# Three reduced-precision products in place of one full one for 44 down projections, the router inside the actor's matrix, an opening that runs by tiles, and GpSimd's follow-up steps planned later

## What is computed

```python
probs = softmax(einsum('bsh,eh->bse', x, router_w))              # 8 experts
a_h = gelu(einsum('bsh,ah->bsa', x, actor_w1) + actor_b1)        # 50 hidden
sampled_k = argmax(clip(a_h @ actor_w2.T + actor_b2, -30, 30)) + 1
rank = argsort(argsort(-probs))
scores = where(rank < sampled_k[..., None], probs, 0.0)
for e in range(8):                                               # I = 336
    g = einsum('bsh,ih->bsi', x, gate_w[e])
    u = einsum('bsh,ih->bsi', x, up_w[e])
    y = einsum('bsi,hi->bsh', silu(g) * u, down_w[e])
    out = out + scores[..., e:e + 1] * y
```

## Time and profile before

| | us |
|---|---|
| median of 3 runs | 499.86 |
| lowest, highest | 499.83, 501.45 |
| the profiled execution | 500.62 |
| its span in the profile | 498.8 |
| PE busy in it | 484.0 |
| DVE, POOL, ACT busy in it | 294.1, 292.1, 243.4 |

### The profile page before, as it was taken

One profiled execution on the slowest core, in us unless ns is written; L12 is line 12 of the kernel. 1 busy time (PEld: TensorE's weight loads), 2 busy tenths in 40 slices (PEclk: granted clock), 3 DMA queues, 4 the chain that ended last, 5 costly groups with the idle time before them and its releaser, 6 DMA issues.

```text
span 498.8 us, 6344 instructions
## 1 busy us (share of the span) xinstructions
PE 484.0 (97%) x2035; PEld 340.1 (68%) x2035; DVE 294.1 (59%) x695; ACT 243.4 (49%) x437; POOL 292.1 (59%) x307
## 2 busy tenths in 40 slices
PE   7798899999999899999999999999999999999997
PEld 7676767677666666676676676667676676666666
DVE  3538343746768795497937985469763334623232
ACT  3185837457624874248742756326671344232221
POOL 4346779338868485464563656365563646655653
PEclk9899999999999999999999999999999999999999
DMA  8700000000000000000000000000000000000000
GB/s 240 237 0 2 0 1 1 0 1 1 1 1 1 1 0 1 0 1 1 0 1 1 0 2 0 1 0 24 0 1 0 1 23 0 0 1 21 1 1 21
DMA packets 7932, 7.36 MB, mean 15 GB/s; under 512 B 732, under 2 KB 7772, under 8 KB 7900
## 3 DMA queue, kind: packets, MB, share of 16 engines
q1 hardware_dynamic: 7900, 6.97, 4.6%
HBM read 5.91 MB, written 1.05 MB: 14 GB/s over the span
## 4 chain that ended last, share of the span: by engine, by line
PE 81%; DVE 2%; ACT 1%; issue 1%; POOL 0%; ACTq 0%; DVEq 0%
PE bank L1157 26%; PE bank L1007 15%; PE bank L1009 14%; PE bank L1008 14%; PE bank L1195 3%; PE bank L1187 1%; PE bank L1111 1%; PE bank L1027 1%; PE bank L1165 1%; PE bank L1207 1%; PE bank L1119 1%; PE bank L1145 1%; PE bank L1098 1%; PE bank L1097 0%; PE bank L1085 0%
## 5 line engine op out<-in xcount | busy, mean ns | idle before, releaser
L574 POOL TENSOR_TENSOR t<-t,sl 128x512 f32<-128x512 f32 x105 | 136.0, 1299 | 109.8 <-DVE t L953 93.4
L691 ACT ACTIVATE sl<-bank 128x512 f32<-128x512 f32 x168 | 99.3, 597 | 150.0 <-PE bank L1009 143.5
L1157 PE MATMUL bank<-t,WD 128*128 128x512 f32 x328 | 162.7, 591 | 0.0
L953 DVE TENSOR_TENSOR t<-bank,sbc 128x512 f32<-128x512 f32 x105 | 72.4, 690 | 93.7 <-PE bank L1009 92.5
L1007 PE MATMUL bank<-xhF,WGh 128*128 128x512 f32 x168 | 103.8, 618 | 3.0 <-ACT sl L691 2.2
L574 POOL TENSOR_TENSOR t<-t,sbc 128x512 f32<-128x512 f32 x63 | 81.9, 1326 | 11.2 <-ACT sbc L685 7.9
L1157 PEld LDWEIGHTS bank<-t,WD 128*128 128x128 f32 x328 | 61.8, 188 | 25.1 <-issue 13.0
L953 DVE TENSOR_TENSOR t<-bank,sl 128x512 f32<-128x512 f32 x63 | 42.8, 685 | 54.7 <-ACT sl L691 24.3
L1007 PE MATMUL bank<-xhF,WUh 128*128 128x512 f32 x168 | 66.5, 396 | 1.3 <-DVE t L953 1.3
L1009 PE MATMUL bank<-xhF,WGl 128*128 128x512 f32 x168 | 66.3, 395 | 0.0
L1009 PE MATMUL bank<-xhF,WUl 128*128 128x512 f32 x168 | 66.0, 393 | 0.0
(11 more groups left out here) (191 smaller groups left out, 636.8 us busy)
## 6 DMA issues: line engine op xcount, KB each, us to landing
stage<-in_gate SPq DMA_DIRECT2D x7, 192.0 KB, 6.1
stage<-in_up SPq DMA_DIRECT2D x7, 192.0 KB, 6.3
WD<-in_down SPq DMA_DIRECT2D x7, 192.0 KB, 6.2
X<-in_x SPq DMA_DIRECT2D x4, 256.0 KB, 5.5
out<-X SPq DMA_DIRECT2D x3, 256.0 KB, 2.3
raw<-in_small SPq DMA_DIRECT2D x1, 388.0 KB, 4.6
out<-X SPq DMA_DIRECT2D x2, 128.0 KB, 1.9
raw<-in_small SPq DMA_DIRECT2D x1, 192.0 KB, 2.7
```

The lines of the kernel that those rows point to most:

```text
L574: pool.tensor_tensor(t2[k % NT2][:, :], t2[k % NT2][:, :], by[:, :], ALU.mult).then_inc(a_done, 1)
L691: act.activation(sl[k % NSL][:, :], bank[k % 2][:, :], ACT.Silu).then_inc(silu_done, 1)
L953: dve.tensor_tensor(t2[k % NT2][:, :], bank[2 + k % 2][:, :], by[:, :], ALU.mult).then_inc(t2_done, 1)
L1157: pe.matmul(OACC[:, :], WD[:, c, :], t2[k % NT2][:, :], start=(c == 0), stop=(c == CH - 1 or k == TAIL[0] - 1))\
```

## The change

**Split down projections.** For 44 of the 168 chunks `down` becomes three float32r matmuls. `plan` picks them in a new function, `halves`: from chunk 54 on (`SPLIT_FROM`), outside `TAIL`, where its running estimate of DVE's load is under a limit and POOL is not too far behind. ACT copies the finished `t2` into `ah` in float32r (step `ah`, 4 buffers), DVE writes the rest `t2 - ah` over `t2`, which it sees as float32r under the name `t2r` (step `al`), and `down` waits for that. The weights are split once, in 7 pieces from slot 27 on: ACT makes `WDh`, POOL makes `WDl` (step `wd`). By block the 44 are 0, 0, 4, 2, 4, 5, 12 and 17; the longest runs of neighbouring chunks are 98 to 101, 127 to 133 and 143 to 163.

**Router in the actor's matrix.** The router's 8 columns move into the columns 64 to 71 of the actor's matrix, whose first 50 are used. `route` is the three wide matmuls alone. A new step `rt` turns the 8 rows of logits into columns by four transposes. The 8 small matmuls, the copies of the router and DVE's sum of three parts go.

**Opening by tiles.** PE waits for `xn` tile by tile. `y` of batch 0 writes four banks and DVE adds each tile when it is there. The first half of `xhF` goes through bank 3 and is copied and split ahead of the second. Chunk 0 starts with the two products that need `xhF` alone. The sums of squares stand ahead of the product beside them, in a bank of their own, and `head_mask` is done half before the first `rstd` and half after.

**POOL's follow-ups later.** What POOL does for `stats`, `ass` and `actk` becomes steps of their own, `rstd`, `apow` and `sx`, that the tables place up to two slots later.

```diff
+SPLIT_FROM, WD_FROM = 2 * CH + 12, CH + 5
...
-F0_STEPS = [(0, "route"), (1, "inner", 0), (2, "rexp"), (3, "inner", 1), (3, "rsum"), (5, "rrank"), (5, "tanh"),
+F0_STEPS = [(0, "route"), (1, "inner", 0), (1, "rt"), (2, "rexp"), (3, "inner", 1), (4, "rsum"), (5, "rrank"), (5, "tanh"),
...
+    def halves(k):
+        room = debt[0] < DEBT_ACT and dve_load[0] < DVE_ROOM + DVE_LOAD["uk"] and pool_free[0] < k + POOL_LEAD
+        for j in split:
+            if ("al", j) not in done and slot_of.get(("ah", j), last) < k:
+                add(("al", j))
+                debt[1] += COST["al"][2]
+        j = seen[0]
+        while j < len(um_end) and um_end[j] + AH_LAG <= k and slot_of["um", j] < k:
+            weights = slot_of.get(("wd", j % CH // WCH), last) + 1 < k
+            if j >= SPLIT_FROM and j not in TAIL and weights and room:
+                split.append(j)
+                add(("ah", j))
...
+                if kind == "ah":
+                    act.wait_ge(a_done, k + 1)
+                    if i >= NAH:
+                        act.wait_ge(down_done, split[i - NAH] + 1)
+                    act.activation(ah[i % NAH][:, :], t2[k % NT2][:, :], ACT.Copy).then_inc(ah_done, 1)
...
+                if kind == "al":
+                    dve.wait_ge(ah_done, i + 1)
+                    dve.tensor_tensor(t2r[k % NT2][:, :], t2[k % NT2][:, :], ah[i % NAH][:, :].bitcast(F32),
+                                      ALU.subtract).then_inc(al_done, 1)
...
                 if kind == "route":
                     m = turn(t)
+                    wh, wl = swide(1)
+                    three(m[:, :], wh, wl, xh[:, :], xl[:, :]).then_inc(m_full[t % 3], 1)
+                if kind == "rt":
+                    wait_free(pe, turn_of["route", n])
+                    m = turn(t)
                     for i in range(NT):
-                        pe.matmul(m[:, o:o + 2 * E], xh[:, a], router[:, :], start=True, stop=True)
-                        r = pe.matmul(m[:, o + 2 * E:o + 3 * E], xl[:, a], router[:, 0:E], start=True, stop=True)
+                        r = pe.transpose(m[:, i * E:i * E + E], xa[R0:R0 + E, i * P:i * P + P], ident[R0:R0 + E, R0:R0 + E])
...
+                    if k in split_at:
+                        r = three(OACC[:, :], WDh[:, c, :], WDl[:, c, :], ah[i % NAH][:, :], t2r[k % NT2][:, :],
+                                  start=(c == 0), stop=(c == CH - 1 or k == TAIL[0] - 1))
```

More of the change, by code:

```diff
@@ L178, in plan, with bank_free @@
     um_end, downs, block_end = [], [0], []
+    split, seen = [], [0]
+    dve_load = [0.0]
+    slot_of = {}
+    wds = [("wd", j) for j in range(CH // WCH)]
+    def bank_free(by):
+        return by in done and (by[0] != "byx" or slot_of[by] < k)
     def ready(s):
@@ L224, in products @@
             j = downs[0]
-            if j < len(um_end) and um_end[j] + AFTER_POOL <= k and (j % CH or j == 0 or block_end[j // CH - 1] + OACC_REST < k):
+            if j in split:
+                due = slot_of.get(("al", j), last) + 1 < k
+            else:
+                due = j < seen[0] and um_end[j] + AFTER_POOL <= k
+            if due and (j % CH or j == 0 or block_end[j // CH - 1] + OACC_REST < k):
                 add(("down", j))
@@ L244, in plan @@
                 th[0] -= th[0] <= k
+        halves(k)
         products(k, 2)
+        if wds and k >= WD_FROM and k % 2:
+            add(wds.pop(0))
+            debt[0] += 0.5
         pe = 2.2
@@ L265, in plan @@
         debt = [max(0.0, act - pe), max(0.0, dve - pe)]
-    assert not any(th[1] for th in threads)
+        dve_load[0] = max(0.0, dve_load[0] - pe)
+    assert not any(th[1] for th in threads) and not wds
     while downs[0] < last:
```

244 lines of the change are left out of this document (168 added, 76 removed).

## The result

The changed kernel takes 503.85 us (median of 6 runs, 502.20 to 503.98), the kernel before 499.85 (499.76 to 501.45): a ratio of 1.0059, 95% interval 1.0044 to 1.0074. The forecast was 487.0, in a range from 483.0 to 491.5. The change makes the kernel 0.6% slower, and the forecast is 17 us off.

What follows compares the result with a forecast made beforehand. PE's work was taken to bound the kernel from chunk 0 on, after an opening chain. 500.62 - 7.3 (splits) - 3.7 (router) - 2.7 (opening) + 0.9 (waits) = 487.8 us, 487.0 against the median; range 483 to 491.5.

Steps and rivals of the forecast that it cites:

- Splits, -7.3 on PE: Down projections of 44 chunks: three float32r matmuls cost 0.69 us against 0.86 for the full down, 7.3 us less.
- the dense stretches don't gain: Rival, chance 0.12: um and al hinder each other, slots of 32 neighbouring chunks stay at 2.24 us, time 492.3.
- POOL goes first: Rival, chance 0.05: in dense stretches POOL gets SBUF ahead of DVE each time, slots take 2.68 us, time 506.4.
- Router, -3.7: Router step in eight blocks: four transposes at 0.44 us replace small matmuls at 0.90, 3.7 us less, bounds 0 and 4.3.
- Opening, -2.7: Chain before chunk 0: Gram matrix 0.7, rs 0.7, y 0.4, start of chunk 0 0.9 us less; bounds 1.0 and 4.7.
- New waits, +0.9, bounds 0 and 3.5: PE's waits on silu and uk: old 3.5 us over 168 chunks, scaled to 44 more operations on ACT and DVE.
- WD's halves, nothing: Seven copies on ACT and seven subtractions on POOL in slots 27 to 39, costed at nothing, POOL busy 261.6 of 438.8 us.
- if that cover were gone: WD's halves: without POOL's spare time they would delay um by up to 9 us of POOL work.
- POOL's steps later, neutral or better: Later placing of POOL's steps might take old waits away, at most 3.5 us.
- A lower granted clock in the main part: Listed among the signs in the profile after that would show the forecast wrong; no size given.
- the fourth rival: The rival POOL goes first, in the dense stretches: 506.4 us, chance 0.05.

Runs made afterwards that it cites:

- e1: The changed kernel without down splits and without the halves of WD, the rest of the change kept: 501.44 us, ratio 1.0042 to the kernel before.
- e7: The changed kernel with tiles on 64 bytes, routing steps early, WD's halves in slots 79 to 91 and splits from chunk 94 on: 496.48 us, ratio 0.9924.
- e12: e7 without splits and without the halves of WD: 500.24 us, ratio 1.0016 to the kernel before.
- e10: e7 with four idle matmuls of 128 columns ahead of the router's transposes in each block: 501.66 us, ratio 1.0029 to the kernel before.
- e9: e7 with 33 more warming matmuls of 128 columns on PE directly ahead of chunk 0: 503.75 us, ratio 1.0074 to the kernel before.
- e4: e1 with the seven pieces of WD's halves made again in slots 27 to 39, used by no down: 504.41 us, ratio 1.0077 to the kernel before.
- e3: e1 with POOL's follow-ups (rstd, apow, sx) back directly behind their first halves: 505.31 us, ratio 1.0104 to the kernel before.
- e2: The changed kernel with POOL's follow-ups (rstd, apow, sx) back directly behind their first halves, 45 splits: 502.88 us, ratio 1.0072 to the kernel before.
- e11: e7 with attention A's rstd and apow back directly behind their first halves and ascale a slot earlier: 495.53 us, ratio 0.9912 to the kernel before.
- e8: The kernel before with one unused 32-byte tile ahead of xhS, shifting the wide halves: 501.91 us, ratio 1.0039 to the kernel before.
- e5: The changed kernel with every SBUF tile rounded up to 64 bytes in place of 32: 501.93 us, ratio 1.0038 to the kernel before.
- e13: e11 with one unused 32-byte tile ahead of xhS in place of rounding all tiles to 64 bytes: 495.41 us, ratio 0.9896 to the kernel before.
- e6: e1 with the routing's steps rt, rexp and rsum in earlier slots: 500.37 us, ratio 1.0002 to the kernel before.
- e14: e13 with the low halves' step xl one slot earlier in F blocks 2 to 7 and the B norms: 492.93 us, ratio 0.9857 to the kernel before.

## Why the prediction was wrong

Point by point, against its own sum of 500.62 - 7.3 - 3.7 - 2.7 + 0.9:

- *Splits, -7.3 on PE.* Right as PE's work: slots of 2.09 us, `al` 0.68 right behind `uk`, PE not bound by DVE in the dense stretches. The rivals "the dense stretches don't gain" and "POOL goes first" did not happen there. But of the 7.3 nothing arrived in the changed kernel (e1), and of 7.1 in e7 3.8 (e12).
- *Router, -3.7.* Right as work (0.41 us for the four). By e10, in e7's order, 0.6 to 0.7 of such a gain arrives.
- *Opening, -2.7.* 3.84 in the profiled executions. 1.46 of it is the 14 warming records, at full clock now; most executions of the kernel before don't have that low stretch, and its median lies 0.77 below the profiled execution, so against the median the gain is 3.84 - 0.77 = 3.1. It counts in full (e9).
- *New waits, +0.9, bounds 0 and 3.5.* **This is the step that failed.** It measured +11.7 us of waits and, with the layout, +3.1 of small gaps. I had priced waits by the number of added operations, at the rate of the old ones. But a wait follows from what stands ahead in the queue of the engine waited for: at 219.15 five products of POOL behind an `rstd` that had waited for DVE, at 121.66 a piece of WD that waited for ACT. ACT's waits for POOL's products went from 2.3 to 16.7 us. Of PE's 11.7 us of added waits 4.3 are there without pieces of WD and splits (e1), 2.6 come with the pieces (e4 against e1) and 4.8 with the splits (the changed kernel against e4). That the old order left PE only 7.2 us because it had been fitted to the old durations is my reading; no run shows it.
- *WD's halves, nothing.* 3.0 to 3.2 us (e4). The cover that I named, POOL's mean load of 60%, is none in a queue that is worked through in order: POOL stood idle for 12.1 us ahead of these pieces, and nothing behind them could start. I had named a price "if that cover were gone" without asking for the cover slot by slot.
- *POOL's steps later, neutral or better.* -2.2 us without splits (e1, e3), +1 with them (e2), +1 for attention's in e7 (e11). The sign hangs on the rest of the order.
- *The layout* had no term. 1.2 us in time (e8), 0.5 won back by e5; 1.6 in the balance of e13.
- *A lower granted clock in the main part* stood in the last paragraph as what would make the prediction wrong, and had no price. It is 1.6 us a stretch, two of them in the median run.

The sum comes out with these: e1 at full clock is 499.9, since what the opening (3.1) and the router (3.5) spare PE is made up by waits (+4.3) and gaps (+2.0); the splits with WD add 0.9 at equal clock; two low stretches add 3.2: 504.0 against 503.85 measured. For the first of these, though, that is a balance and not a cause. By e9, in e7's order, a shift of chunk 0 leaves the waits behind it as they are, so in e1 something else in the change costs as much as opening and router bring. The layout is some 1.2 us of it (e8). The late follow-ups are not it (without them, e3, it is 2.2 us more), and the slots of the routing's steps are not it (e6). The rest is open, and the router's new chain is the candidate that no run takes out.

"Only the fourth rival lies above 497.4" was the other mistake: the time came out above it without that rival. Its mechanism, POOL ahead of DVE slot after slot where `um` and `al` alternate, did not happen, and the long lockout of e11 isn't in the changed kernel either. The waits came from queues in which products and small steps stand behind something that is late, for which the prediction had no rival.

What stays open: why stretches at the lower clock come in some executions and not in others. In the profiled executions they followed waits of 1.5 us or more: at 39 to 40 and at 51 to 52 us in e1 and e4, at 49 us in e13 and the changed kernel, at 167 and 350 us in e14. But e7, e11 and e12 have the same wait of 1.77 us at 49.2 to 49.5 and kept the full clock. And why the four spacings depend on how the tiles lie; e8 and e13 show only that they do.

## What to carry to other kernels

Cost an added operation by the backlog of its engine in its own slots, not by the engine's mean load over the kernel, and ask who is queued behind it. When PE is nearly always busy, don't count on all that is taken from it: here between nothing (e1) and 0.7 (e10) of it arrived in the blocks, and all of it ahead of them (e9). Ask of every added operation what it waits for, since all that stands behind it in its queue waits too, and try the parts of a change apart and late in the kernel before all together. When tiles move, look at the spacing of undisturbed matmuls in both traces before explaining anything else.

## What the runs showed of the hardware

- A DVE operation with both inputs in SBUF can wait for a whole run of POOL multiplications: 5.01 us for an operation of 0.19 us, four products of 1.25 us (e11). It need not: at the same place it was let in behind the first of four, in 1.40 us (e14).
- The position of float32r tiles modulo 64 bytes changes the spacing of undisturbed matmuls: 0.922 us for four before, 0.930 when shifted by 32 bytes, 0.928 with all tiles on 64 bytes, 0.921 with the wide halves on 64 and the others 32 past.
- Stretches at half the granted clock inside a main part in which PE is busy for 95 to 97% of the span, each some 1.6 us: 499.9, 501.4, 503.2 and 504.6 us for none to three of them in one kernel (e1).
- A full float32 matmul of 128 columns is two records of 0.11 us, 0.22 in all (e9: 66 records for 33).
- Four transposes of 8 rows and 128 columns of weights are recorded with 0.41 us in all.
